# GpSimd takes over four elementwise steps of each update of h, and the value buffers go from two to four

## What is computed

```
# layer 0: a_sum from the context (lora_A), router over 8 experts
w = softmax(x @ router_W.T + router_b)
a_sum = einsum('bsh,arh->bsr', x, lora_A)
out = x + 0.5 * sum_n w[n] * (a_sum @ lora_B[n].T)
h = nan_to_num(out, nan=0.0, posinf=10000.0, neginf=-10000.0)
# layer 1
Q = h @ Wq.T + bq;  K = ctx @ Wk.T + bk;  V = ctx @ Wv.T + bv
attn = softmax(Q K^T / sqrt(32), masked)
z = h + (attn V) @ Wo.T + bo
return layernorm(z) * ln_g + ln_b
```

## Time and profile before

| what | us |
|---|---|
| median of 3 runs | 709.3 (708.08 to 709.73) |
| the profiled execution, its own time | 709.77 |
| its span | 708.0 |
| PE busy | 671.1 (95%) |
| DVE busy | 472.5 (67%) |
| ACT busy | 295.7 (42%) |
| POOL busy | 256.7 (36%) |

### The profile page before, as it was taken

One profiled execution on the slowest core, in us unless ns is written; L12 is line 12 of the kernel. 1 busy time (PEld: TensorE's weight loads), 2 busy tenths in 40 slices (PEclk: granted clock), 3 DMA queues, 4 the chain that ended last, 5 costly groups with the idle time before them and its releaser, 6 DMA issues.

```text
span 708.0 us, 10732 instructions
## 1 busy us (share of the span) xinstructions
PE 671.1 (95%) x3615; PEld 574.2 (81%) x3615; DVE 472.5 (67%) x916; ACT 295.7 (42%) x891; POOL 256.7 (36%) x247
## 2 busy tenths in 40 slices
PE   9999859999889999999998999999999999999995
PEld 7878647888678887888887898888888888888884
DVE  5777665456625567346735667888888888888744
ACT  4522222211214013221205666766666666666511
POOL 0213320212202221202242334466666666666552
PEclk9999969999979999999999999999999999999998
DMA  9875575313656437671255699352445254523211
GB/s 304 298 239 162 156 232 135 125 56 93 201 194 229 159 89 231 216 255 61 96 168 124 265 383 324 82 164 84 153 106 151 90 165 120 152 87 119 96 68 75
DMA packets 101062, 115.18 MB, mean 163 GB/s; under 512 B 41360, under 2 KB 75280, under 8 KB 101008
## 3 DMA queue, kind: packets, MB, share of 16 engines
q1 hardware_dynamic: 101008, 114.50, 49.9%
HBM read 68.33 MB, written 46.14 MB: 162 GB/s over the span
## 4 chain that ended last, share of the span: by engine, by line
PE 64%; issue 16%; DMA 5%; SPq 5%; POOL 5%; DVE 4%; ACT 1%; POOLq 0%; DVEq 0%; ACTq 0%
PE ps L537 19%; PE ps L538 18%; PE ps L539 18%; POOL h_t L1116 4%; PE ps L679 4%; PE ps L588 3%; SPq L450 2%; DMA stage<-BT 1%; DMA bo_b<-bo 1%; DMA qb<-q_cols 1%; PE ps L620 1%; SPq L443 1%; DMA stage<-WkT 1%; DVE w_lo L743 1%; SPq L458 0%
## 5 line engine op out<-in xcount | busy, mean ns | idle before, releaser
L1116 POOL TENSOR_TENSOR h_t<-pos,neg 128x512 f32<-128x512 f32 x32 | 48.5, 1514 | 189.6 <-DVE neg L828 185.4
L537 PE MATMUL ps<-act_hi,w_hi 128*128 128x512 f32 x256 | 103.4, 404 | 1.7 <-DVE w_lo L743 1.4
L537 PE MATMUL ps<-wo_hi,cx_hi 128*128 128x512 f32 x256 | 104.5, 408 | 0.0
L1046 ACT ACTIVATE s_sb<-s_sb,s_min 128x64 f32<-128x64 f32 x256 | 86.3, 338 | 39.3 <-DVE s_min L870 39.3
L538 PE MATMUL ps<-act_lo,w_hi 128*128 128x512 f32 x256 | 101.1, 395 | 0.0
L539 PE MATMUL ps<-act_hi,w_lo 128*128 128x512 f32 x256 | 101.0, 395 | 0.0
L539 PE MATMUL ps<-wo_hi,cx_lo 128*128 128x512 f32 x256 | 100.3, 392 | 0.0
L538 PE MATMUL ps<-wo_lo,cx_hi 128*128 128x512 f32 x256 | 100.2, 391 | 0.0
L1136 POOL TENSOR_TENSOR s_sb<-s_sb,s_min 128x256 f32<-128x256 f32 x64 | 39.3, 614 | 139.7 <-DVE s_min L870 139.7
L1018 ACT ACTIVATE act_hi<-h_t 128x512 fp32r<-128x512 f32 x32 | 20.2, 632 | 166.5 <-DVE h_t L834 166.5
L865 DVE SCALAR_TENSOR_TENSOR s_sb<-ps,mask_f 128x512 f32<-128x512 f32 x64 | 44.2, 691 | 52.0 <-PE ps L539 50.4
(11 more groups left out here) (110 smaller groups left out, 1549.2 us busy)
## 6 DMA issues: line engine op xcount, KB each, us to landing
q_cols<-q_sb SPq DMA_DIRECT2D x32, 512.0 KB, 4.8
qb<-q_cols SPq DMA_DIRECT2D x64, 256.0 KB, 3.4
x_sb<-xT SPq DMA_DIRECT2D x32, 256.0 KB, 3.1
h_rows<-hn_sb SPq DMA_DIRECT2D x32, 256.0 KB, 3.2
output_weights<-wo_sb SPq DMA_DIRECT2D x32, 256.0 KB, 2.7
z_sb<-h_rows SPq DMA_DIRECT2D x16, 512.0 KB, 4.1
out<-z_sb SPq DMA_DIRECT2D x15, 512.0 KB, 2.8
stage<-WkT SPq DMA_DIRECT2D x8, 512.0 KB, 6.2
```

The lines of the kernel that those rows point to most:

```text
L537: pe.matmul(dst, lh, rh, start=(first and j == 0), stop=False)
L1046: act.activation(s_sb[c % 4][:, h, :], s_sb[c % 4][:, h, :], ACT.Exp, bias=s_min[c % 2][:, h:h + 1], scale=-1.0, accum_out=s_sum[c % 2][:, ...
L1116: pool.tensor_tensor(h_t[m % 3][:], pos[m % 2][:], neg[m % 2][:], ALU.add).then_inc(sign_ready, 1)
```

## The change

- `kv_sb` becomes four buffers with a semaphore each; `values_out` on ACT no longer waits for a store. The buffers lie in slots 2 and 3 of the Q weight, so the Q weight blocks 3 and 2 are split last, each when two of the buffers have been stored, and the first Q half runs over k = 0, 1, 5, 6, 7, 4, 3, 2.
- The turns of K stand in pairs: 0 and 1 behind the third query block of batch 0, 2 and 3 behind the fourth (before: 0, then 1, then 2 and 3).
- The key bias is loaded first of the small loads and has its own semaphore.
- The raw tiles of the output weight are loaded during batch 0 (`output_weight_in`), and `rows` of chunk 6 and 7 (with line 811) stand ahead of `output_weight` in the list.
- `zero` loads four tiles of Q ahead of the keys, and the 1 MB of output weight moves from step 3 to step 6.
- The mask, the positive and the negative part move from DVE to POOL, ahead of the addition.

```
-Q_FIRST = (0, 1, 3, 4, 5, 6, 7, 2)
+Q_FIRST = (0, 1, 5, 6, 7, 4, 3, 2)
...
-    beside = {0: {1: rows(0, 6) + split("Q", 6), 2: [("turn", 0)] + split("Q", 7), 3: rows(0, 7) + [("turn", 1)],
-                  4: [("turn", 2), ("turn", 3)], 5: [("mask",), ("route", 1)], 6: split("Q", 2)}}
+    beside = {0: {0: split("Q", 7), 1: rows(0, 6) + split("Q", 4), 2: [("turn", 0), ("turn", 1)], 3: rows(0, 7) + [("turn", 2), ("turn", 3)],
+                  4: split("Q", 3), 5: [("mask",), ("route", 1)] + split("Q", 2)}}
...
             def zero():
...
-                load_q(0)
-                load_q(1)
+                for n in range(4):
+                    load_q(n)
...
         @block.vector
...
             def update(i, c):
...
                 dve.scalar_tensor_tensor(t_c, ps_up[c % 2], LORA_SCALE, t_c, ALU.mult, ALU.add).then_inc(t_ready, 1)
-                wait(dve, sign_ready, m - 1)
-                wait(dve, h_ready, m - 1)
-                dve.wait_ge(t_ready, m + 1)
-                dve.tensor_scalar(finite[m % 2][:], t_c, 0.0, 0.0, ALU.mult, ALU.is_equal).then_inc(f_ready, 1)
-                dve.tensor_scalar(pos[m % 2][:], t_c, 0.0, 1e4, ALU.is_gt, ALU.mult).then_inc(sign_step, 1)
-                dve.tensor_scalar(neg[m % 2][:], t_c, 0.0, -1e4, ALU.is_lt, ALU.mult).then_inc(sign_step, 1)
...
             def values_out():
                 act.wait_ge(v_mm, KC)
                 for g in range(4):
-                    wait(act, kv_stored[g % 2], 32 * (g // 2))
-                    act.activation(kv_sb[g % 2][:, 0, :], ps_q[g], ACT.Copy).then_inc(kvhi_done, 1)
+                    act.activation(kv_sb[g][:, 0, :], ps_q[g], ACT.Copy).then_inc(kvhi_done, 1)
...
-            def signs(m):
+            def update(i, c):
+                m = KC * i + c
+                t_c = x_sb[:, c, :]
+                pool.wait_ge(t_ready, m + 1)
+                pool.tensor_scalar(pos[m % 2][:], t_c, 0.0, 1e4, ALU.is_gt, ALU.mult).then_inc(sign_step, 1)
+                pool.tensor_scalar(neg[m % 2][:], t_c, 0.0, -1e4, ALU.is_lt, ALU.mult).then_inc(sign_step, 1)
+                wait(pool, h_ready, m - 1)
+                pool.tensor_scalar(finite[m % 2][:], t_c, 0.0, 0.0, ALU.mult, ALU.is_equal).then_inc(f_ready, 1)
                 pool.wait_ge(sign_step, 2 * m + 2)
```

More of the change, by code:

```diff
@@ L94, in first_phase @@
         out += [("values", c)] + up(0, c - 1, *(split("V", c + 3) if c + 3 < KC else split("Q", c + 3 - KC)))
-    out += [("values", KC - 1), ("values_out",)] + split("Q", 3) + up(0, 6, *split("Q", 4)) + up(0, 7, *split("Q", 5))
-    beside = {0: {1: rows(0, 6) + split("Q", 6), 2: [("turn", 0)] + split("Q", 7), 3: rows(0, 7) + [("turn", 1)],
-                  4: [("turn", 2), ("turn", 3)], 5: [("mask",), ("route", 1)], 6: split("Q", 2)}}
+    out += [("values", KC - 1), ("values_out",)] + up(0, 6, *split("Q", 5)) + up(0, 7, *split("Q", 6))
+    beside = {0: {0: split("Q", 7), 1: rows(0, 6) + split("Q", 4), 2: [("turn", 0), ("turn", 1)], 3: rows(0, 7) + [("turn", 2), ("turn", 3)],
+                  4: split("Q", 3), 5: [("mask",), ("route", 1)] + split("Q", 2)}}
     for i in range(1, NB):
-        beside[i] = {n: [("output_weight", KC * (i - 1) + n)] if i < NB - 1 else [] for n in range(KC)}
-        beside[i][0] += rows(i, 6)
-        beside[i][1] += rows(i, 7)
+        beside[i] = {n: rows(i, 6 + n) if n < 2 else [] for n in range(KC)}
         if i < NB - 1:
+            for n in range(KC):
+                beside[i][n] += [("output_weight", KC * (i - 1) + n)]
             beside[i][2] += [("route", i + 1)]
@@ L118, in first_phase @@
             if k == 0 and i == 0:
-                out += [("expand", 1, 1)]
+                out += [("expand", 1, 1), ("output_weight_in",)]
             if k >= late:
@@ L244, in xattn_kernel @@
         bk_b = at("bk_b", [P, H], AT_W_HI + 4096)
-        kv_sb = [at(f"kv_sb{k}", [P, 2, HALF], (AT_W_HI, AT_W_LO)[k] + 2 * 4096, F32R) for k in range(2)]
+        kv_sb = [at(f"kv_sb{k}", [P, 2, HALF], (AT_W_HI, AT_W_LO)[k % 2] + (2 + k // 2) * 4096, F32R) for k in range(4)]
         k_rows = at("k_rows", [P, 2, H], AT_QS)
@@ L292, in xattn_kernel @@
         kvhi_done, kvlo_done = sem("kvhi_done"), sem("kvlo_done")
-        kv_stored = [sem(f"kv_stored{k}") for k in range(2)]
+        kv_stored = [sem(f"kv_stored{k}") for k in range(4)]
         al_mm, route, route_exp = sem("al_mm"), sem("route"), sem("route_exp")
@@ L460, in zero @@
             def zero():
-                for k in range(2):
-                    sp.wait_ge(kv_stored[k], 192)
+                for k in range(4):
+                    sp.wait_ge(kv_stored[k], 96)
                 sp.wait_ge(sign_ready, ALL)
                 sp.wait_ge(h_ready, ALL)
-                load_q(0)
-                load_q(1)
+                for n in range(4):
+                    load_q(n)
                 sp.wait_ge(zeroed, 2)
@@ L486, in step @@
                 c = s % KC
-                if live(s + 1, CHUNKS) and s >= 1:
+                if live(s + 1, CHUNKS) and s >= 3:
                     load_q(s + 1)
@@ L980, in split @@
                     act.wait_ge(k_copied, 4)
-                if what == "Q" and k == 2:
-                    for j in range(2):
-                        act.wait_ge(kv_stored[j], 192)
-                if what == "Q" and k >= 3:
+                if what == "Q" and k in (2, 3):
+                    for j in (2 * k - 4, 2 * k - 3):
+                        act.wait_ge(kv_stored[j], 96)
+                if what == "Q" and k >= 4:
                     act.wait_ge(v_mm, KC)
```

41 lines of the change are left out of this document (21 added, 20 removed).

## The result

The changed kernel takes **835.37 us** (median of 4 runs, 834.46 to 835.57), against 708.69 (708.0 to 709.73) of the kernel before in the same session: the ratio is 1.178, 95% interval 1.176 to 1.180. It is 127 us slower, where 706.5 with a range of 698.5 to 731 was forecast. Direction and size were wrong.

What follows compares the result with a forecast made beforehand. PE sets the end, so its waits before 400 us decide, and for them the update loop through POOL. Terms -0.7, +2.6, -2.5, -0.1, +1.4 and -3.5 sum to -2.8: 706.5 us against the median, range 698.5 to 731.

Steps and rivals of the forecast that it cites:

- the price P: Time of one new POOL operation in the update loop: 0.62 us from POOL's select row, range 0.45 to 1.045.
- Rival 2: The update loop through POOL becomes the bound: slower, 727 to 731 us, 748 at 1.045 us per operation; 38% together.
- The loop formula: DVE's update loop through POOL takes 4.25 us plus three POOL operations: 6.11 us, against PE's period of 5.93.
- The prediction's own sums: Whole kernel: -2.8 us, 706.5, at 0.62 us per POOL operation; +38 at 1.045; about 7 to 9 per 0.1 us.
- The blocking beside a split: V projection loops: a split's 0.92 us blocking moves from the addition to POOL's first operation, so it cancels.
- End of V: End of the V projection: ACT waiting for no store gains 4.8 us, six longer loops cost 4.1; net -0.7.
- Turns: Turns of K: the second turn waits 2.6 us, the fourth 1.5; +2.6 us, bounds +1.5 and +5.2.
- End of batch 1: End of batch 1's updates: the copy of h ends earlier despite longer loops; -2.5 us, low clock stays.
- End of batch 2: End of batch 2's updates: copy of h done at 280.9 against PE's restart at 281.19; -0.1 us.
- End of batch 3: End of batch 3's updates: copy of h done at 361.3, PE comes by at 359.93; a new stall, +1.4 us.
- Seam: At the seam, four Q tiles ahead remove two waits and low clock, keys come later; -3.5 us, bounds -5.2, -1.5.
- the first rival: POOL works at plain-write rate, 0.45 us per operation, update loop under PE's period; 697.4 us; 10%.

Runs made afterwards that it cites:

- experiment 5: Changed kernel with its three new POOL operations as multiply-and-add pairs instead of pairs with a comparison; 707.7 us, ratio 0.999 to the kernel before.
- experiment 1: Changed kernel with the mask and both sign parts back on DVE, everything else kept; 699.98 us, ratio 0.988 to the kernel before.
- 4: Changed kernel with other arithmetic in POOL's three operations: single comparisons for positive part and mask, multiply and add for negative part; 768.72 us.
- 6: Changed kernel with POOL's operations as a max/min pair, a comparison with multiply in two halves, and multiply and add; 802.98 us.
- experiment 9: Changed kernel with mask, signs and their addition all on DVE, so POOL has no part in the update; 699.83 us, ratio 0.987.
- Experiment 3: Changed kernel with both sign parts back on DVE and only the mask on POOL; 707.58 us, ratio 0.997 to the kernel before.
- 11: Changed kernel with mask, signs, addition on DVE, K turns one per block, two Q tiles ahead of keys, POOL's zeroing held; 693.97 us, ratio 0.977.
- 7: Changed kernel with mask and signs back on DVE, and the K turns one to a query block, two splits behind them; 694.81 us, ratio 0.982.
- experiment 10: Changed kernel with mask, signs and addition on DVE, and POOL's zeroing held until the last h is ready; 695.15 us, ratio 0.980.
- experiment 8: Changed kernel with mask and signs back on DVE, and only two Q tiles loaded ahead of the keys; 697.86 us, ratio 0.986.

## Why the prediction was wrong

**The step that failed is the price P and its bounds.** P was taken from the select's row and bounded above by the two-input addition, on the ground that an input more must cost more. It measured 1.93, 1.85 times the upper bound. The kind of function counted, and no row of POOL had a comparison with a number in it: the select compares a pattern of indices with zero, not the data. The forecast took the row for "a comparison" in name. For arithmetic the same estimate was right (0.62), which is luck: nothing in the select's row told of a multiply and an add. The step to take instead: an operation whose function is not in the trace has no upper bound from rows of other functions, and the range has to say so. Rival 2 named the mechanism, with 38%, but its range ended at 748, since it used the same bound.

**The loop formula** was right: 4.25 + the sum of POOL's operations is 0.1 to 0.15 too long at each of four points of the table. The start-to-start times are a little under the durations. The prediction's own sums, 706.5 at 0.62 and +38 at 1.045, rise by 9.6 us for each 0.1 us of P (not the 7 to 9 that it states). An estimate along this slope to P = 1.93 is 832 us; 835.4 was measured. So the path was right too, and the one number put into it was not.

**The blocking beside a split** was predicted to move to POOL's first operation and to stay at 0.92 us. It did. Beside a split line 1113 takes 2.83, 0.90 more than 1.93:

```profile
60.98 2.83 POOL L1113 TENSOR_SCALAR pos<-x_sb 128x512 f32<-128x512 f32 x1 [2.91 <-DVE x_sb L826]
```

**The other terms** are judged on experiment 5, where P is what they assumed. Its gaps of PE against those of before:

```profile
77.08 0.63 PE L622 MATMUL ps<-ident,h_t 128*128 128x128 f32 x4 [1.16 <-DVE hn_sb L815]
...
94.44 1.09 PE L622 MATMUL ps<-ident,h_t 128*128 128x128 f32 x4 [7.14 <-DVE hn_sb L815]
113.19 1.09 PE L576 MATMUL ps<-ident,k_rows 128*128 128x128 f32 x4 [4.51 <-DVE kv_sb L757]
121.48 0.63 PE L576 MATMUL ps<-ident,k_rows 128*128 128x128 f32 x4 [1.50 <-DVE kv_sb L757]
...
199.04 0.63 PE L622 MATMUL ps<-ident,h_t 128*128 128x128 f32 x4 [2.53 <-DVE hn_sb L815]
367.76 0.36 PE L539 MATMUL ps<-kbd_hi,qb 128*128 128x256 f32 x1 [1.69 <-issue]
381.43 0.78 PE L539 MATMUL ps<-act_hi,w_hi 128*128 128x512 f32 x1 [1.89 <-DVE q_sb L842]
```

- End of V: predicted -0.7. With the gap of 0.78 at 83.94, 9.1 us in all against 10.88: -1.8. Right in kind: the gain of 4.8 (4.83 in experiment 1) was mostly eaten.
- Turns: predicted +2.6, between 1.5 and 5.2. (Its terms for DVE add up to t0 + 16.1 and not 16.7, so it should have said +2.0.) 6.0 against 1.50: +4.5. Near the upper bound; the second of a pair waits as described, and the clock behind it was not in the term.
- End of batch 1: predicted -2.5, with the low clock kept. 2.53, and 0.16 at 187.16, against 6.37: -3.7, and the low clock is gone (1.00 from 190 to 220 us, 0.83 before). Too small a gain.
- End of batch 2: predicted -0.1; the gap of 1.47 fell to 0.22: -1.2. End of batch 3: predicted +1.4; the gap is 0.23: +0.2. In the main both follow from a loop of 5.98 instead of 6.11, which is 0.8 to 0.9 us over six or seven updates.
- Seam: predicted -3.5, between -5.2 and -1.5. The waits are 1.69 + 1.89 + 0.4 against 2.9: **+1.1**, outside its bounds. This is the second step that failed. The low clock did not go either: 0.64 in the 4 us behind the second wait, 0.63 before. The keys did come later as said, by somewhat more than 1.2. But I took the two waits for Q tiles as removed, and did not ask what is late next behind them. It was the low parts of Q.

The gaps add up to -0.9, PE's work is 0.6 shorter, and the span of experiment 5 is 1.7 us shorter than that before. That 707.7 lies so near to 706.5 is thus in part luck: a seam forecast 4.6 us too low and turns forecast 1.9 too low stand against the end of V and the three batches, together forecast 4.6 too high.

The prediction cited the Trainium skill (GPSIMD Engine Reference, section Engine selection) for one-input operations at "roughly line-rate". The traces come near to it for multiply and add (0.62 us, where VectorE takes 0.42 for a pair with a comparison) and disagree for comparisons, max and min (1.50 to 1.93). The prediction had set this rule beside the first rival and did not build on it.

## What to carry to other kernels

Price an operation on an engine by a row with the same function on it, not by one with the same number of inputs. Where there is none, an upper bound from other rows is no bound. In a loop that passes through several engines, it is the sum around the loop that counts, not any engine's share: POOL was half idle and cost 127 us. And when a wait is removed, ask what was being done during it, and whether an instruction was held in its place by the queue that you now empty.

## What was not expected of the hardware

- On GpSimd, 128x512 in single precision: multiply with add 0.62 us (experiment 5); one comparison 1.50 (4); a comparison with multiply, or max with min, 1.93 (the changed kernel, 6). On VectorE the mask and the signs take 0.42 to 0.43 each (1).
- Zeroing by GpSimd held a one-input operation of VectorE for 4.8 us, over three zeroings in a row and not only the one under way (experiment 9). The operation before it on DVE, with one input in PSUM and one in SBUF, ran beside a zeroing in its usual 0.68. The Trainium skill (SBUF — State Buffer, section Who interferes with whom) has the second of such a pair blocked for the first one's whole length. This trace agrees, and adds that the operation did not get in between one zeroing and the next. Experiment 3 does not agree: an operation of VectorE that started 0.04 us after one of GpSimd (1.92 us) was held for only 0.4.
- A wait of 1.41 us ahead of 64 small matmuls was followed by some 12 us at 1.2 GHz in one trace and by none in another (experiments 11 and 7). A wait of 2.4 us at the first turn was followed by a clock of 0.61 over 4 us in experiment 10 and by 1.00 in experiment 8. Differences of 2 to 5 us between such kernels can be of this kind, and not of the edit.
